# A graph layer on one core: another order of the work ahead of the first product with h

## The reference, cut to what matters

```
h = relu(layernorm(x))                      # x: 8192 x 256 float32
mask = adj > 0                              # adj: 8192 x 8192 int32
agg = mask @ h / max(row_sum(mask), 1)
self_f = h @ W_self + b_self
nb_f = agg @ W_nb + b_nb
out = x + relu(concat(self_f, nb_f) @ W_comb + b_comb)
```

## Time and profile before

| | us |
|---|---|
| median of 3 runs (1001.43 to 1001.74) | 1001.66 |
| the profiled execution | 1001.76 |
| its span, first to last instruction | 1000.0 |
| TensorE busy | 989.9 |
| VectorE busy | 673.9 |
| ScalarE busy | 585.0 |
| GpSimd busy | 30.5 |

### The profile page before, as it was taken

One profiled execution on the slowest core, in us unless ns is written; L12 is line 12 of the kernel. 1 busy time (PEld: TensorE's weight loads), 2 busy tenths in 40 slices (PEclk: granted clock), 3 DMA queues, 4 the chain that ended last, 5 costly groups with the idle time before them and its releaser, 6 DMA issues.

```text
span 1000.0 us, 14269 instructions
## 1 busy us (share of the span) xinstructions
PE 989.9 (99%) x4696; PEld 460.5 (46%) x4696; DVE 673.9 (67%) x1163; ACT 585.0 (59%) x675; POOL 30.5 (3%) x73
## 2 busy tenths in 40 slices
PE   7999999999999999999999999999999999999998
PEld 4555444444444444444444444444444444444443
DVE  6886677986776666766667666676666766667711
ACT  5888886775655556655556555565555655556500
POOL 2332000000000000000000000000000000000000
PEclk9999999999999999999999999999999999999999
DMA  9621399999888898888988888888888888888600
GB/s 344 251 85 43 140 421 371 416 420 377 320 316 321 312 341 317 319 322 312 342 312 322 322 313 336 318 322 322 312 328 328 323 315 321 321 326 326 218 16 10
DMA packets 58994, 295.04 MB, mean 295 GB/s; under 512 B 6624, under 2 KB 24160, under 8 KB 26208
## 3 DMA queue, kind: packets, MB, share of 16 engines
q1 hardware_dynamic: 58976, 294.81, 78.6%
HBM read 286.39 MB, written 8.39 MB: 295 GB/s over the span
## 4 chain that ended last, share of the span: by engine, by line
PE 98%; DMA 1%; DVE 0%; SPq 0%; issue 0%
PE pair_ps L360 89%; PE pair_ps L351 8%; PE turn_ps L333 1%; DMA self_f<-in_x_dram 1%; PE pair_ps L381 0%; DVE x_again L439 0%; SPq L195 0%; SPq L193 0%; DVE z L505 0%; DVE fold L502 0%; DVE x_again L442 0%; DVE part L485 0%; DVE part L482 0%; DVE x_again L488 0%; SPq L177 0%
## 5 line engine op out<-in xcount | busy, mean ns | idle before, releaser
L360 PE MATMUL pair_ps<-z,mask_t 128*128 128x512 f16 x4096 | 885.8, 379 | 0.0
L290 ACT ACTIVATE mask<-mask 128x2048 uint8<-128x2048 uint8 x256 | 488.0, 1908 | 341.4 <-DVE mask_t L430 341.4
L360 PEld LDWEIGHTS pair_ps<-z,mask_t 128*128 128x128 fp8e4 x4096 | 396.2, 98 | 475.7
L430 DVE STREAM_TRANSPOSE mask_t<-mask 128x512 uint32<-128x512 uint32 x256 | 181.7, 710 | 219.8 <-PE pair_ps L360 214.3
L424 DVE TENSOR_SCALAR mask<-stage 128x2048 uint8<-128x2048 int32 x256 | 308.1, 1203 | 6.0 <-DMA stage<-in_adj_dram 5.9
L351 PE MATMUL pair_ps<-mask_t 128*128 128x512 f16 x384 | 87.8, 379 | 0.0
L351 PEld LDWEIGHTS pair_ps<-mask_t 128*128 128x128 f16 x384 | 37.6, 98 | 38.6
L290 ACT ACTIVATION_READ_ACCUMULATOR mask<-mask 128x1 f32 x256 | 48.1, 188 | 0.0
L482 DVE SCALAR_TENSOR_TENSOR part<-pair_ps,rdeg,self_f 128x256 f32<-128x256 f32 x64 | 31.0, 484 | 15.7 <-DVE rdeg L477 11.9
L269 ACT ACTIVATE self_f<-self_f,x_again 128x256 f32<-128x256 f32 x64 | 35.0, 605 | 8.7 <-POOL x_again L260 8.7
L447 DVE SCALAR_TENSOR_TENSOR mask_t<-turn_ps,mask_t 128x512 f16<-128x512 f32 x32 | 21.8, 681 | 19.3 <-ACT mask_t L276 19.3
(11 more groups left out here) (31 smaller groups left out, 93.0 us busy)
## 6 DMA issues: line engine op xcount, KB each, us to landing
stage<-in_adj_dram SPq DMA_DIRECT2D x256, 1024.0 KB, 5.9
self_f<-in_x_dram SPq DMA_DIRECT2D x16, 512.0 KB, 15.4
x_again<-in_x_dram SPq DMA_DIRECT2D x64, 128.0 KB, 5.3
out_dram<-x_again SPq DMA_DIRECT2D x64, 128.0 KB, 5.1
z<-in_L_gnn_W_comb_dram SPq DMA_DIRECT2D x2, 256.0 KB, 4.8
z<-in_L_gnn_W_self_dram SPq DMA_DIRECT2D x1, 256.0 KB, 3.6
z<-in_L_gnn_W_nb_dram SPq DMA_DIRECT2D x1, 256.0 KB, 4.5
z<-in_L_gnn_b_comb_dram SPq DMA_DIRECT2D x1, 128.0 KB, 6.4
```

The source lines that it names most:

```text
L290: act.activation(mask[:, a, :], mask[:, a, :], ACT.Copy, accum_out=deg_part[:, n, a:a + 1]).then_inc(counted, 1)
L360: mm = pe.matmul(acc[n], bytes_of[:, :, s], z16[:, SUB * e + s, :], start=(e == 0 and s == 0), stop=(e == CHUNKS - 1 and s == SUB - 1))
L430: dve.transpose(mask_t[:, n, :, a, :], src).then_inc(transposed, 1)
```

## The change

SP issues x chunk 0 and the two blocks of weights 1, ScalarE's queue those of weights 0. TensorE runs 8 products of the identity with itself, whose result nobody reads, while the weights are on the way. The statistics go from VectorE to GpSimd pair by pair instead of chunk by chunk, and the negated mean is taken on VectorE. The two weight products are split high and low in between the first pairs. The bias product is made behind the products of pair 0, as two columns of 128 values out of 8 products of one column; VectorE spreads these over 128 columns, and two products with the identity behind those of pair 1 turn them into rows. The tile `ones`, which nobody read, goes.

```
+        def load_w(eng, n):
+            dst, w = ((ws_t, w_self_t), (wn_t, w_nb_t))[n]
+            eng.dma_start(dst, w...).then_inc(w_loaded[n], DONE)
+            eng.dma_start(wc[:, n * HALVES:(n + 1) * HALVES, :], w_comb[...]...).then_inc(w_loaded[n], DONE)
 SP:
             load_x(0)
-            (the four weight blocks)
+            load_w(sp, 1)
             load_x(1)
 GpSimd:
-            for e in range(CHUNKS):
-                pool.wait_ge(aggr_done, SUB * (e + 1))
-                pool.tensor_scalar(var_s[:, e % 2, :], mean_var[:, e, :, 1], EPS, ...)
-                pool.tensor_scalar(minus_mean[:, e % 2, :], mean_var[:, e, :, 0], -1.0, ...)
-                pool.tensor_tensor(rstd[:, e, :], var_s[:, e % 2, :], power, ALU.pow)
-                pool.tensor_tensor(shift[:, e, :], minus_mean[:, e % 2, :], rstd[:, e, :], ALU.mult)
+            for p in range(PAIRS):
+                e, s0 = divmod(2 * p, SUB)
+                two = slice(s0, s0 + 2)
+                pool.wait_ge(aggr_done, 2 * (p + 1))
+                pool.tensor_scalar(var_s[:, e % 2, two], mean_var[:, e, two, 1], EPS, ...)
+                pool.tensor_tensor(rstd[:, e, two], var_s[:, e % 2, two], power[:, 0:2], ALU.pow)
+                pool.tensor_tensor(shift[:, e, two], minus_mean[:, e % 2, two], rstd[:, e, two], ALU.mult)
 ScalarE:
-                act.wait_ge(shift_ready, e + 1)
+                act.wait_ge(shift_ready, j + 1)          (in norm(j))
-            norm(0)
-            norm(1)
-            (w_high of 0 and 1)
+            load_w(act, 0)
+            w_high_of(0)
+            norm(0)
+            w_high_of(1)
             high_of_h(0)
+            norm(1)
             norm(2)
 TensorE:
             pe.wait_ge(ident_ready, 1)
+            for _ in range(WARMING):                     (8)
+                pe.matmul(turn_ps[0][:, 0:P], ident, ident, start=True, stop=True)
             (the two weight products)
             turn(0)
             turn(1)
-            pe.wait_ge(wide_ready, 2 * HALVES)
-            for m in range(2 * HALVES):
-                mm = pe.matmul(pair_ps[2][:, 0, 0:D], b_wide[:, m, :], wc[:, m, :], ...)
-            mm.then_inc(c_product, 1)
             for j in range(PAIRS):
                 if j + 2 < PAIRS:
                     turn(j + 2)
                 project(j)
+                if j == 0:
+                    pe.wait_ge(b_loaded, 2 * DONE)
+                    for half in range(HALVES):
+                        for m in range(2 * HALVES):
+                            mm = pe.matmul(pair_ps[2][:, 0, half:half + 1], wc[:, m, half * P:(half + 1) * P],
+                                           b_cols[:, m:m + 1], start=(m == 0), stop=(m == 2 * HALVES - 1))
+                    mm.then_inc(c_column, 1)
+                if j == 1:
+                    pe.wait_ge(wide_ready, HALVES)
+                    for half in range(HALVES):
+                        mm = pe.matmul(pair_ps[2][:, 1, half * P:(half + 1) * P], c_wide[:, half, :], ident, ...)
+                    mm.then_inc(c_product, 1)
 VectorE:
+                if p >= 4:                               (at the end of stats_of(p))
+                    dve.wait_ge(shift_ready, p - 3)
+                dve.wait_ge(aggr_done, 2 * (p + 1))
+                dve.tensor_scalar(minus_mean[:, e % 2, s0:s0 + 2], mean_var[:, e, s0:s0 + 2, 0], -1.0, ...)
-            for p in range(4):
-                stats_of(p)
-            (fold: 4 copies)
-            (b_wide: 4 copies)
-            w_low(0)
-            w_low(1)
-            low_of_h(0)
-            for p in range(4, 6):
-                stats_of(p)
-            dve.wait_ge(c_product, 1)
-            dve.tensor_tensor(c_row[:, :], pair_ps[2][:, 0, 0:D], bc_row, ALU.add).then_inc(c_ready, 1)
+            stats_of(0)
+            w_low(0)
+            stats_of(1)
+            w_low(1)
+            low_of_h(0)
+            for p in range(2, 6):
+                stats_of(p)
+            (fold: 4 copies)
             for j in range(PAIRS + 2):
                 if j + 1 < PAIRS:
                     low_of_h(j + 1)
+                if j == 1:
+                    (waits c_column; 2 copies of a column over 128 columns: c_wide)
+                if j == 2:
+                    dve.wait_ge(c_product, 1)
+                    dve.tensor_tensor(c_row[:, :], pair_ps[2][:, 1, 0:D], bc_row, ALU.add).then_inc(c_ready, 1)
```

More of the change, by code:

```diff
@@ L42 @@
 RING = 3
+WARMING = 8
 MASK_STEPS = (5, 11, 17, 23)
@@ L136, in graph_layer @@
         w_product = sem("w_product")
+        c_column = sem("c_column")
         c_product = sem("c_product")
@@ L172, in chunk_of @@
             return t[:, SUB * e:SUB * (e + 1), :]
+        def load_w(eng, n):
+            dst, w = ((ws_t, w_self_t), (wn_t, w_nb_t))[n]
+            eng.dma_start(dst, w.rearrange("(h p) n -> p h n", p=P)).then_inc(w_loaded[n], DONE)
+            eng.dma_start(wc[:, n * HALVES:(n + 1) * HALVES, :],
+                          w_comb[n * D:(n + 1) * D, :].rearrange("(h p) n -> p h n", p=P)).then_inc(w_loaded[n], DONE)
         @block.sync
@@ L244, in _ @@
             pool.memset(power, -0.5).then_inc(zeroed, 1)
-            pool.memset(ones, 1.0).then_inc(zeroed, 1)
             pool.memset(eight[:, :], SUM_HELD).then_inc(zeroed, 1)
-            pool.wait_ge(zeroed, 4)
+            pool.wait_ge(zeroed, 3)
             pool.affine_select(out=ident, in_=ident, compare_op=ALU.not_equal, fill=1.0, base=0,
                                pattern=[[-1, P]], channel_multiplier=1).then_inc(ident_ready, 1)
-            for e in range(CHUNKS):
-                pool.wait_ge(aggr_done, SUB * (e + 1))
-                pool.tensor_scalar(var_s[:, e % 2, :], mean_var[:, e, :, 1], EPS, H_SCALE ** -2,
-                                   ALU.add, ALU.mult).then_inc(var_ready, 1)
[L255 to L260, removed]
+            for p in range(PAIRS):
+                e, s0 = divmod(2 * p, SUB)
+                two = slice(s0, s0 + 2)
+                pool.wait_ge(aggr_done, 2 * (p + 1))
+                pool.tensor_scalar(var_s[:, e % 2, two], mean_var[:, e, two, 1], EPS, H_SCALE ** -2,
+                                   ALU.add, ALU.mult).then_inc(var_ready, 1)
+                pool.wait_ge(var_ready, p + 1)
+                pool.tensor_tensor(rstd[:, e, two], var_s[:, e % 2, two], power[:, 0:2], ALU.pow).then_inc(rstd_ready, 1)
+                pool.wait_ge(rstd_ready, p + 1)
+                pool.wait_ge(negated, p + 1)
+                pool.tensor_tensor(shift[:, e, two], minus_mean[:, e % 2, two], rstd[:, e, two], ALU.mult
+                                   ).then_inc(shift_ready, 1)
         @block.scalar
@@ L265, in norm @@
                 e, s0 = divmod(2 * j, SUB)
-                act.wait_ge(shift_ready, e + 1)
+                act.wait_ge(shift_ready, j + 1)
                 for s in (s0, s0 + 1):
@@ L291, in count, with w_high_of @@
                                accum_out=deg_part[:, n, a:a + 1]).then_inc(counted, 1)
-            norm(0)
-            norm(1)
-            for n in range(2):
+            def w_high_of(n):
                 act.wait_ge(w_product, n + 1)
@@ L369, in _ @@
             pe.wait_ge(ident_ready, 1)
+            for _ in range(WARMING):
+                pe.matmul(turn_ps[0][:, 0:P], ident, ident, start=True, stop=True)
             for n, w_t in enumerate((ws_t, wn_t)):
@@ L387, in _ @@
                 project(j)
+                if j == 0:
[8 more added lines that the diff above has]
+                    for half in range(HALVES):
+                        mm = pe.matmul(pair_ps[2][:, 1, half * P:(half + 1) * P], c_wide[:, half, :], ident,
+                                       start=True, stop=True)
+                    mm.then_inc(c_product, 1)
             def tile(r, n, counts=()):
@@ L442, in stats_of @@
                     dve.bn_aggr(mean_var[:, e, s, :], stats[:, e % 2, s, :]).then_inc(aggr_done, 1)
+                if p >= 4:
+                    dve.wait_ge(shift_ready, p - 3)
+                dve.wait_ge(aggr_done, 2 * (p + 1))
+                dve.tensor_scalar(minus_mean[:, e % 2, s0:s0 + 2], mean_var[:, e, s0:s0 + 2, 0], -1.0, None, ALU.mult
+                                  ).then_inc(negated, 1)
             def low_of_h(j):
@@ L516, in _ @@
                     low_of_h(j + 1)
+                if j == 1:
+                    dve.wait_ge(c_column, 1)
+                    for half in range(HALVES):
+                        dve.tensor_copy(c_wide[:, half, :], pair_ps[2][:, 0, half:half + 1].to_broadcast([P, P])
+                                        ).then_inc(wide_ready, 1)
+                if j == 2:
+                    dve.wait_ge(c_product, 1)
+                    dve.tensor_tensor(c_row[:, :], pair_ps[2][:, 1, 0:D], bc_row, ALU.add).then_inc(c_ready, 1)
                 if j >= 2:
```

8 lines of the change are left out of this document (1 added, 7 removed).

## The result

The changed kernel takes 1009.05 us (median of 6 runs, 1008.76 to 1009.78), the kernel before 1001.7 (6 runs beside it): a ratio of 1.0073, 95% interval 1.0060 to 1.0086. It is slower, as forecast, but by 7.35 us where 3.4 were forecast (1005.1), outside the range of 1002.9 to 1006.8.

A forecast was written before the change was run, and what follows sets the result against it. TensorE bounds the kernel, so a later first product with h and added TensorE work count in full: +1.0 start, +1.8 column, +0.45 broadcast back, +0.2 c_row = +3.45 us, giving 1005.1 us, range 1002.9 to 1006.8.

The forecast's parts named there:

- the main reading: The bias product L381 lies in a TensorE hole, costing some 0.2 us there; the change takes it out of that hole.
- 1.8 + 0.45 + 0.2 us: On TensorE behind pairs 0 and 1: one-column products 1.8, two products turning them back 0.45, stall for c_row 0.2 us.
- the new order delays the start: VectorE takes pair 2's statistics only behind low_of_h(0), so the first product with h starts at 15.95, 1.0 us later.
- The power on two values: GpSimd's power in the statistics, on 2 instead of 4 values: between 0.2 and 1.04 us, taken as 0.62.
- both products run at the fast level: Idle products raise TensorE's clock, so the second weight product ends at 9.95 us in place of 11.32.
- the forecast left both blocks where they were: W_comb's two blocks still land at 5.85 and 7.96 us, since bytes and not issue times set the second landing.
- this sharing for x chunk 0: x chunk 0 shares the DMA engines with two weight blocks and may land up to 1.4 us later than 4.18.
- rival (c): Clock stays low through the weight products; second ends at 11.3, start 17.3, +4.8, total 1006.5 us; chance 0.10.
- c_row's stall: project(2) on TensorE waits for VectorE's c_row: 0.2 us of new stall (0 to 0.5).

The follow-up runs named there:

- The runs with all the assumed conditions: Changed kernel with weight blocks issued by SP in the old order, 10 idle products, and idle products in TensorE's two holes: 1005.45 us, ratio 1.0030.
- The version with 14 idle products: Changed kernel with loads by SP in the old order, idle products in TensorE's two holes, and 14 ahead of the weight products: 1006.55 us, ratio 1.0045.

## Why the prediction was right in its sign and wrong in its size

*Right: the main reading.* L381 had stood in a hole; out of it, it costs. Forecast 1.8 + 0.45 + 0.2 us; in the profile L399 moves its successor by 23.87 - 22.16 = 1.71, L405 by 0.44, and project(2) waits 0.34 for c_row (28.15 - 27.37 - 0.44). Alone in the kernel before it costs the same, 2.51.

*Right: the new order delays the start.* From the end of the weight products to norm(2)'s end the forecast had 15.25 - 9.95 = 5.30 us, the profile 17.62 - 12.26 = 5.36. The old order on VectorE gives 3.4 us back, of which about 1.0 is the clock in pair 0. The power on two values took 0.70 us (forecast 0.62).

*Wrong: "both products run at the fast level", so the second ends at 9.95.* It ended at 12.26, 2.3 us later. The run with the old order on VectorE parts the two causes, since its weights landed at the same time and its clock was up: there the products end at 10.54. So 0.6 us is the landing and 1.7 the low clock. The landing: the forecast left both blocks where they were, with the end bound by the second one. Now the first block of W_comb landed at 1.23 + 5.55 = 6.8 us instead of 5.85, though issued 0.4 us earlier, and the second at 1.65 + 5.7 = 7.4 instead of 7.96, issued 1.0 earlier. The first came late enough to push both products. The likely reason is that the first product's two blocks, W_self and its half of W_comb, now share the DMA engines with blocks issued beside them by SP; with SP as the only issuer they landed earlier in five profiles of eight, so this isn't settled. The forecast had this sharing for x chunk 0 (up to 1.4 us later; it came 0.4 later, 4.57) and not for the weights. The Trainium skill (DMA: Bandwidth & Descriptors, section "Queues, rings and completion order") says that each DMA engine takes turns between the queues that have work for it; the two landings agree. The low clock is the forecast's rival (c), which had 1 in 10.

*Wrong, and in no rival: that the clock, once up, stays.* The delayed start makes two holes of 2.5 and 1.7 us, and the clock is low from 17.2 to 20.6. Transposes of pair 2 and products of pair 0 take 0.27 and 0.99 us more (0.97 for 0.70 from norm's end, 3.58 for 2.59). Idle products in the holes take this away. c_row's stall was 0.34 us, for 0.2. The sum is then: start +1.0 by the forecast, +2.3 for the weight products, +0.3; pair 0 +1.0; bias 2.5: 7.1 us.

The runs with all the assumed conditions gave 1005.45 for 1005.1, and the terms one by one came out within 0.15 us: they were sound, the conditions were not. Whether the median run met them no trace shows; the one profiled, at 1008.49, did not. The version with 14 idle products says the same by its profile: its first product with h came 1.37 us later than forecast, and 1006.79 - 1.37 is 1005.4. The range went wrong where it took each rival alone. (c) gave 1006.5; with the products ending at 12.26 and not 11.3, and with the second fall, 1.3 us, it would have been 1008.7. Late landing, late rise and second fall came together.

Open: what decides in one execution whether 8 idle products lift the clock; why a hole of 2.8 us (the bias column in the kernel before) let it stand and shorter ones didn't; and how much of the late landing is the second queue. On the first, the two groups of runs with the old order on VectorE suggest that it parts them too, but there is one profile for each version, so this is shown for profiled executions only.

## What to carry to other kernels

Work in a hole of the bounding engine costs little where it is (here some 0.2 us, behind pair 0 2.5); before moving it, ask what is in front of it once the hole is gone. When a change makes new holes ahead of the bounding engine's first work, count its clock too: a row of the kernel before shows only the level that its own holes allow. A second queue is not free of cost: here the last weight block landed 0.6 us sooner, and the block that was needed first 0.9 us later. Landings vary by more than that between executions, so one profile doesn't judge a change of issue.

## What the runs showed of the hardware that I had not expected

- Equal work, other moment: with 8 idle products from 1.59 to 5.4 and weight products from 6.82 on, 16 matmuls ran from 6.9 to 10.2 in one execution and 8 in another; the recorded rise of the clock was at 5.77 and at 10.34 us.
- Holes of 2.5 and 1.7 us with 0.65 us of transposes between were followed by a fall of the granted clock to 0.50, from 17.2 to 20.6 us; so was one of 2.0 us ahead of the weight products (8.4 to 11.8, while the engine was busy). One of 2.82 us was not.
- GpSimd's power took 1.04 us on four values a partition and 0.70 on two: half the values save a third of the time.
- A float32 product of one column behind its own weight load costs 0.107 us for each of its two instructions (1.71 for 16), against 0.03 for the f16 one behind a long product.
- With the same issue times, W_comb's first block landed 4.2 to 4.5 us after its issue in five executions, 6.0 in two (the two versions with all the forecast's conditions) and between them in one, which moves the weight products by up to 1.7 us.
